# Attention factors of four edge groups at once and one-hot matrices built on GpSimd, in the second graph layer's sums

## The reference, cut to what matters

```python
def _L1_gnn_ref(h, W, a_l, a_r, src, dst):
    N, IN_FEAT, OUT_FEAT, HEADS, E = (2500, 1024, 256, 4, 40000)
    NEG_SLOPE = 0.2
    z = jnp.einsum('ni,hif->nhf', h, W)
    el = jnp.einsum('nhf,hf->nh', z, a_l)
    er = jnp.einsum('nhf,hf->nh', z, a_r)
    e = jax.nn.leaky_relu(el[src] + er[dst], NEG_SLOPE)
    m = jax.ops.segment_max(e, dst, num_segments=N)
    ex = jnp.exp(e - m[dst])
    s = jax.ops.segment_sum(ex, dst, num_segments=N)
    alpha = ex / s[dst]
    out = jax.ops.segment_sum(alpha[:, :, None] * z[src], dst, num_segments=N)
    return out.reshape(N, HEADS * OUT_FEAT)
```

## Time and profile before

| | us |
|---|---|
| median of 3 runs | 3157.28 |
| lowest and highest of them | 3145.21, 3158.06 |
| span of the profiled execution | 3172.0 |
| of it, from the first to the last product of the sums (L1508 to L1550) | 1878.5 to 2518.0 |
| busy over the whole span: TensorE, VectorE, ScalarE, GpSimd | 2750.2, 2445.8, 1667.2, 1658.5 |

### The profile page before, as it was taken

One profiled execution on the slowest core, in us unless ns is written; L12 is line 12 of the kernel. 1 busy time (PEld: TensorE's weight loads), 2 busy tenths in 40 slices (PEclk: granted clock), 3 DMA queues, 4 the chain that ended last, 5 costly groups with the idle time before them and its releaser, 6 DMA issues. The chain is left out here.

```text
span 3172.0 us, 49827 instructions
## 1 busy us (share of the span) xinstructions
PE 2750.2 (87%) x13389; PEld 2152.8 (68%) x13389; DVE 2445.8 (77%) x5315; ACT 1667.2 (53%) x3377; POOL 1658.5 (52%) x1473
## 2 busy tenths in 40 slices
PE   4999969999997998477877789999999789499997
PEld 3788734444445776355656568888888678388886
DVE  8656769999997676356666589999999986677875
ACT  3555623333334525122222259999999754366664
POOL 1788757766663562555555525555555332034333
PEclk9999989999998999789898899999999889599999
DMA  5433489999991031001010138888888854588886
GB/s 182 115 94 101 159 304 342 340 345 342 345 335 50 7 135 54 13 17 22 16 22 15 22 140 309 304 311 306 309 308 309 257 192 162 203 228 230 230 235 160
DMA packets 197470, 600.30 MB, mean 189 GB/s; under 512 B 42763, under 2 KB 52354, under 8 KB 196174
## 3 DMA queue, kind: packets, MB, share of 16 engines
q0 software_dynamic: 135040, 429.23, 42.5%
q1 hardware_dynamic: 62286, 169.29, 15.3%
HBM read 513.25 MB, written 84.95 MB: 189 GB/s over the span
## 5 line engine op out<-in xcount | busy, mean ns | idle before, releaser
L663 POOL DMA_INDIRECT g_rows<-z_rows,edge_src x704 | 731.6, 1039 | 513.4 <-PE g_totals L1550 227.7
L1132 POOL DMA_INDIRECT shared<-el_rows,edge_src x352 | 337.1, 958 | 317.3 <-DVE t_largest L1379 164.1
L1512 PE MATMUL g_sums<-g_rows,g_share 128*128 128x256 f32 x1760 | 446.0, 388 | 2.9 <-issue 1.6
L704 ACT ACTIVATE g_scaled_hi<-g_rows,edge_weight_sorted 128x1024 fp32r<-128x1024 f32 x176 | 202.6, 1151 | 361.7 <-DMA g_rows<-z_rows,edge_src 346.7
L1379 DVE TENSOR_REDUCE t_largest<-t_masked 128x4 f32<-128x512 f32 x352 | 234.4, 685 | 160.9 <-PE t_masked L1218 112.3
L718 PE MATMUL g_sums<-g_rows,g_share 128*128 128x512 f32 x704 | 333.4, 596 | 21.1 <-DMA g_rows<-z_rows,edge_src 21.1
L1512 PEld LDWEIGHTS g_sums<-g_rows,g_share 128*128 128x128 f32 x1760 | 308.8, 191 | 37.0 <-issue 2.4
L331 POOL DMA_INDIRECT edge_list<-payload,row_i x196 | 259.9, 1326 | 125.8 <-issue 116.5
L739 DVE SCALAR_TENSOR_TENSOR g_scaled_lo<-g_rows,edge_weight_sorted,g_scaled_hi 128x1024 fp32r<-128x1024 f32 x176 | 225.6, 1282 | 54.1 <-ACT g_scaled_hi L704 39.2
L1216 PE MATMUL t_masked<-t_never,t_apart 128*128 128x512 f32 x352 | 158.1, 449 | 109.0 <-DVE t_largest L1379 88.3
L1485 ACT ACTIVATE g_scaled_hi<-g_rows,g_factor 128x256 fp32r<-128x256 f32 x528 | 227.9, 494 | 15.1 <-DMA g_rows<-z_rows,edge_src 9.7
(11 more groups left out here) (407 smaller groups left out, 7553.3 us busy)
## 6 DMA issues: line engine op xcount, KB each, us to landing
e_raw<-in_L_ffn_rw_dram SPq DMA_DIRECT2D x28, 1024.0 KB
g_rows<-z_rows,edge_src POOLq DMA_INDIRECT x704
g_place_of<-place_rows SPq DMA_DIRECT2D x44, 256.0 KB
z_rows<-z_zout SPq DMA_DIRECT2D x20, 512.0 KB
x_rows<-x_all SPq DMA_DIRECT2D x20, 512.0 KB
z_rows<-t_zout SPq DMA_DIRECT2D x20, 512.0 KB
s_x<-x_rows SPq DMA_DIRECT2D x20, 512.0 KB
xn_rows<-s_rows SPq DMA_DIRECT2D x10, 1024.0 KB
```

What stands on the lines that cost most here:

```text
L663: pool.indirect_dma_start(out=r.rows[:, slot, :], out_offset=None, in_=table, in_offset=bass.IndirectOffsetOnAxis(ap=g.src[:, i * GT + q:i ...
L1132: q.indirect_dma_start(out=g.edge_el[:, n, :], out_offset=None, in_=g.el, in_offset=bass.IndirectOffsetOnAxis(ap=g.src[:, n:n + 1], axis=0 ...
L1512: t.matmul(sums[:, it.buf(2), h // 2, h % 2 * HF:(h % 2 + 1) * HF], share[:, it.buf(2), n, :], r.rows[:, it.buf(4) * GT + q, h * HF:(h + 1 ...
```

## The change

- The reads of the place broadcast stay, but the one-hot matrices `comes` are made on GpSimd, by one comparison per group (128 x 256, bf16 to fp32r), between the gathers; ScalarE's Square and Relu go. `comes` has four buffers now. GpSimd makes `comes` of group i + 4 after the gathers of group i.
- `of_edge` has two PSUM banks of four groups each. VectorE's reduction, addition, leaky relu and subtraction, and ScalarE's exponential, run once in four groups on four times the data.
- The lags grow: VectorE's step s has `goes` of s - 5 and, when that is the first of four, the scores of s - 5 to s - 2; the share and `scaled_lo` are of s - 6, the sums on TensorE of s - 7, `x_all` of s - 8. `factor` has eight buffers.
- The share of head 1, column 0, moves from VectorE to ScalarE (two and three shares become one and four).
- A turn of `in_steps` is 8 groups on TensorE and VectorE too, and ScalarE writes two turns out ahead of its loop.

```diff
-        comes = a.sb("g1_comes", [P, 2, GT, P], F32R)
+        comes = a.sb("g1_comes", [P, 4, GT, P], F32R)
-        of_edge_bank = a.psum("g1_of_edge", [P, HALF])
+        of_edge_banks = a.psum("g1_of_edge", [P, 2, HALF])
+        SCORED, SCALED, SUMMED, KEPT = AHEAD + 1, AHEAD + 2, AHEAD + 3, AHEAD + 4
...
         @block.gpsimd
-            gather_groups(nc, pool, r, g, g.z1)
+            def gather(i):
+                at_least(pool, r.multiplied, i - 3)
+                for c in range(GT):
+                    slot = i % 4 * GT + c
+                    q.indirect_dma_start(
+                        out=r.rows[:, slot, :], out_offset=None, in_=g.z1,
+                        in_offset=bass.IndirectOffsetOnAxis(ap=g.src[:, i * GT + c:i * GT + c + 1], axis=0),
+                    ).then_inc(r.gathered[slot], 16)
+            def come(i):
+                if i >= NG:
+                    return
+                if i % AHEAD == 0:
+                    pool.wait_ge(place_in[i // AHEAD % 2], (i // AHEAD // 2 + 1) * 16)
+                at_least(pool, of_edge_ready, i - 3)
+                at = i % AHEAD * GT * P
+                q.tensor_scalar(comes[:, i % 4].rearrange("p q n -> p (q n)"),
+                                place_of[:, i // AHEAD % 2, at:at + GT * P], lane[:, 0:1], None,
+                                ALU.is_equal).then_inc(comes_ready, 1)
+            for i in range(NG):
+                gather(i)
+                if i == 0:
+                    pool.wait_ge(lane_ready, 1)
+                if i < AHEAD:
+                    come(2 * i)
+                    come(2 * i + 1)
+                else:
+                    come(i + AHEAD)
...
         @block.scalar
-                    s.activation(apart[:, m, :], place_of[:, it.off // AHEAD, at:at + GT * P], ACT.Square,
-                                 bias=minus_lane[:, 0:1]).then_inc(apart_ready, 1)
...
-                    s.activation(comes[:, m].rearrange("p q n -> p (q n)"), apart[:, m, :], ACT.Relu, bias=one[:, 0:1],
-                                 scale=-1.0).then_inc(comes_ready, 1)
-                it = item(2)
+                it = item(SCALED)
...
-                    act.wait_ge(factor_ready, it.i + 1)
+                    act.wait_ge(factor_ready, it.turn(AHEAD) + 1)
...
-                    for n, q, h in ((2, 0, 2), (3, 0, 3), (4, 1, NATIVE)):
+                    for n, q, h in ((1, 0, 1), (2, 0, 2), (3, 0, 3), (4, 1, NATIVE)):
...
-                it = item(1)
-                if it:
-                    k = it.buf(4)
-                    act.wait_ge(score_ready, it.i + 1)
-                    at_least(act, r.multiplied, it.i - 3)
-                    s.activation(factor[:, k].rearrange("p q h -> p (q h)"), score[:].rearrange("p q h -> p (q h)"),
-                                 ACT.Exp).then_inc(factor_ready, 1)
-            in_steps(act, NG, 2 * AHEAD, body, lead=1)
+                it = item(SCORED)
+                if it and it.off % AHEAD == 0:
+                    f = it.buf(2 * AHEAD)
+                    act.wait_ge(score_ready, it.turn(AHEAD) + 1)
+                    at_least(act, r.multiplied, it.i - AHEAD)
+                    s.activation(factor[:, f:f + AHEAD].rearrange("p k q h -> p (k q h)"),
+                                 score[:].rearrange("p q h -> p (q h)"), ACT.Exp).then_inc(factor_ready, 1)
+            in_steps(act, NG, 2 * AHEAD, body, lead=2)
...
         @block.tensor
-                it = item(3)
+                it = item(SUMMED)
...
-                    at_least(pe, score_ready, it.i)
+                    if it.off % AHEAD == 0:
+                        at_least(pe, score_ready, it.turn(AHEAD) - 1)
...
-            in_steps(pe, NG, 4, body, lead=2)
+            in_steps(pe, NG, 2 * AHEAD, body, lead=2)
...
         @block.vector
-                it = item(4)
+                it = item(KEPT)
...
-                new, it, old = item(0), item(1), item(2)
+                new, old = item(SCORED), item(SCALED)
+                it = new if new and new.off % AHEAD == 0 else None
                 if it:
-                    dve.wait_ge(of_edge_ready, it.i + 1)
-                    st.done(v.tensor_reduce(of_node[:], of_edge.rearrange("p q (a h) -> p q h a", a=2), AX.X, ALU.add))
+                    f = it.buf(2 * AHEAD)
+                    dve.wait_ge(of_edge_ready, it.i + AHEAD)
+                    st.done(v.tensor_reduce(of_node[:], of_edge[:, f // AHEAD].rearrange("p k q (a h) -> p (k q) h a", a=2),
+                                            AX.X, ALU.add))
...
-                    shared_out(0)
+                    v.tensor_scalar(share[:, m, 0, :], goes[:, k, 0, :].bitcast(F32), factor[:, f, 0, 0:1], None,
+                                    ALU.mult).then_inc(share_v, 1)
...
-                    shared_out(1).then_inc(share_v, 1)
...
-            in_steps(dve, NG, 4, body, st, 3, lead=2)
+            in_steps(dve, NG, 2 * AHEAD, body, st, 6, lead=2)
```

More of the change, by code:

```diff
@@ L109, in turn, with in_steps @@
         return self.j * (self.unroll // count) + self.off // count
-def in_steps(eng, count, unroll, body, steps=None, per_step=0, lead=1):
+def in_steps(eng, count, unroll, body, steps=None, per_turn=0, lead=1):
     turns = count // unroll
@@ L133, in in_steps @@
         if steps:
-            steps.n = entry + (j - lead) * (unroll * per_step)
+            steps.n = entry + (j - lead) * per_turn
         for b in range(unroll):
@@ L137, in in_steps @@
     if steps:
-        steps.n = entry + (turns - 1 - lead) * unroll * per_step
+        steps.n = entry + (turns - 1 - lead) * per_turn
     for b in range(unroll):
@@ L1452, in _ @@
         def _(pool):
-            gather_groups(nc, pool, r, g, g.z1)
+            q = nc.gpsimd
+            def gather(i):
[25 more added lines that the diff above has]
+                    come(i + AHEAD)
         @block.scalar
@@ L1524, in body @@
                 if it:
-                    m = it.buf(2)
                     pe.wait_ge(comes_ready, it.i + 1)
                     pe.wait_ge(node_ready, it.i + 1)
-                    at_least(pe, score_ready, it.i)
+                    if it.off % AHEAD == 0:
+                        at_least(pe, score_ready, it.turn(AHEAD) - 1)
                     for q in range(GT):
-                        mm = t.matmul(of_edge[:, q, :], comes[:, m, q, :], node[:, it.buf(4)].rearrange("p a h -> p (a h)"),
-                                      start=True, stop=True)
+                        mm = t.matmul(of_edge[:, it.buf(2 * AHEAD) // AHEAD, it.buf(AHEAD), q, :], comes[:, it.buf(4), q, :],
+                                      node[:, it.buf(4)].rearrange("p a h -> p (a h)"), start=True, stop=True)
                     mm.then_inc(of_edge_ready, 1)
-                it = item(3)
+                it = item(SUMMED)
                 if it:
@@ L1559, in _ @@
             st.link(v.tensor_tensor(lanes[:], g.ident[:], g.iota1[:], ALU.mult))
-            st.link(v.tensor_reduce(minus_lane[:], lanes[:], AX.X, ALU.add))
-            st.done(v.tensor_scalar(minus_lane[:], minus_lane[:], -1.0, None, ALU.mult))
-            st.done(v.memset(one[:], 1.0))
+            v.tensor_reduce(lane[:], lanes[:], AX.X, ALU.add).then_inc(lane_ready, 1)
             st.link(v.tensor_copy(parts[:, :, 0, :], g.scores[:]))
@@ L1588, in body @@
                 if it:
-                    at_least(dve, factor_ready, it.i)
+                    at_least(dve, factor_ready, it.turn(AHEAD))
                     dve.wait_ge(v_done, st.n)
-                    st.done(v.tensor_tensor(score[:], g.edge_el[:, bass.ds(it.i * GT, GT), :],
+                    st.done(v.tensor_tensor(score[:], g.edge_el[:, bass.ds(it.i * GT, AHEAD * GT), :],
                                             of_node[:, :, HEADS:2 * HEADS], ALU.add))
@@ L1599, in body @@
                                                    op0=ALU.mult, op1=ALU.max))
-                def shared_out(h):
-                    return v.tensor_scalar(share[:, old.buf(2), h, :], goes[:, old.buf(4), 0, :].bitcast(F32),
-                                           factor[:, old.buf(4), 0, h:h + 1], None, ALU.mult)
                 if old:
+                    k, m, f = old.buf(4), old.buf(2), old.buf(2 * AHEAD)
                     dve.wait_ge(goes_ready, old.i + 1)
-                    dve.wait_ge(factor_ready, old.i + 1)
+                    dve.wait_ge(factor_ready, old.turn(AHEAD) + 1)
                     at_least(dve, r.multiplied, old.i - 1)
-                    shared_out(0)
+                    v.tensor_scalar(share[:, m, 0, :], goes[:, k, 0, :].bitcast(F32), factor[:, f, 0, 0:1], None,
+                                    ALU.mult).then_inc(share_v, 1)
                 if it:
@@ L1618, in body @@
                         ins = v.scalar_tensor_tensor(out=scaled_lo[:, m, cols], in0=r.rows[:, k * GT + 1, cols],
-                                                     scalar=factor[:, k, 1, h:h + 1],
```

(1 more changed line is left out.)

30 lines of the change are left out of this document (12 added, 18 removed).

## The result

The changed kernel takes 3170.6 us (median of 20 runs, 3156.03 to 3178.35) where the kernel before takes 3150.3 (median of 20 runs, 3139.95 to 3162.32): a ratio of 1.0059, 95% interval 1.0047 to 1.0070. It is slower by 20 us, where I had forecast 13 us less. The spans of the two profiled executions say nothing on this, 3167.8 after and 3172.0 before: the stage's first gather starts at 1855.3 us in the one and at 1869.3 in the other, and all code ahead of it is the same. So I compare the stage alone.

What follows compares the result with a forecast made beforehand. VectorE was taken as the bound at 3.62 us a group, TensorE next at 3.53. Over 176 groups -16, late rows +2, start +1: -13 us, so 3144 from the 3157.28 median; range 3136 to 3178, 8 in 10.

Steps and rivals of the forecast that it cites:

- What bounds the kernel before: In this stage VectorE sets the pace at 3.62 us a group; TensorE, at 3.53, waits 0.09 for it.
- VectorE's own work: On VectorE, a share removed and scores done once in four groups: 3.62 falls to 3.17 us a group.
- The price of the comparison: On GpSimd, one comparison of 256 elements taken as 0.40 us, with 0.23 and 0.75 as ends.
- GpSimd's gathers: On GpSimd, a pair of gathers with the gaps ahead of them takes 2.73 us a group.
- The holds: GpSimd and VectorE blocking each other: 0.1 us a group for VectorE (3.27), 0.2 for GpSimd (3.33).
- the phase: Comparison starts 2.7 us after the gathers start, runs when VectorE's low parts are through; late engines fall back into this timing.
- The slack of the comparison: Between the comparison's end on GpSimd and TensorE's use of it: about 0.5 us.
- The start: Before the first sums, four comparisons and a second pair of gathers: 0 to 4.3 us, taken as 1.
- Late rows: ScalarE waiting for gathered rows, as TensorE sees it: 0 to 10 us, taken as 2.
- B: Rival: dear comparison after the gathers makes GpSimd (+19 us) or VectorE (+53) the bound; 3176 to 3210 us; chance 0.2.
- Rival A: Comparison holds VectorE 0.40 us every group, 3.57 to 3.62; time 3151 to 3160; chance 0.23 together with another rival.

Runs made afterwards that it cites:

- Column 1 first: Gather of column 1 issued ahead of column 0's; ratios to kernel before: on that kernel 1.0009, changed kernel 1.006, comparison on VectorE 0.9927, scores only 0.9943.
- the scores alone: Changed kernel, but the one-hot matrices stay on ScalarE (Square and Relu) and the shares stay two and three; ratio 0.9982 to the kernel before.
- The repetition: The changed kernel run again unaltered, on the chip of three later runs; ratio 1.0036 to the kernel before, stage 664.8 us.

## Why the prediction was wrong

**The outcome.** 3170.6 us lies inside the range of 3136 to 3178, but that is no credit to the mechanism: TensorE did not become the bound, the change went the other way, and the median before was 3150.3, 7 lower than the 3157.28 that I had worked from.

**What bounds the kernel before: right.** VectorE at 3.62, with TensorE 0.09 behind it. TensorE's own pace was measured as 3.52 where it is the bound. Column 1 first, worth nothing on the kernel before, confirms that rows were not what it waited for.

**VectorE's own work: right.** 3.17 us a group had been worked out. With a comparison of its own of 0.38 us, a slot of about 0.32 by its timeline (2154.80 to 2155.12), it is busy 446 of 450 us at a pace of 3.52, which is 3.49 a group, 3.17 and 0.32, and TensorE keeps its 3.52.

**The price of the comparison: this step failed.** The sum had GpSimd at 3.33 us a group, under TensorE's 3.53, with a comparison of 0.40 us, and 0.23 and 0.75 as its ends. It is 0.91 undisturbed, beyond the upper end, and GpSimd's stream came to 3.67. I had chosen by the number of inputs, a cast at 0.88 ns an element and a select of 128 elements at 0.29 us. The two-input additions, 2.15 ns an element by the same rows, are the nearer neighbours of 2.5. And 0.75, from two inputs, had been taken as the upper end for one; no row said that one input cannot cost more.

**GpSimd's gathers: over-counted.** 2.73 us a pair had 0.30 ahead of every gather and 1.17 for the first. Behind a comparison the gap is 0.17, the comparison follows a gather after 0.03, and the first gather takes 1.02: 0.17 + 1.02 + 0.31 + 0.95 + 0.02 = 2.47. With 0.91 that is 3.38, still under TensorE's 3.53. So by this sum the price alone, though more than twice my value, would not have made GpSimd the bound.

**The holds: right for GpSimd, too low for VectorE.** I took 0.2 us for GpSimd and 0.1 for VectorE. The comparison takes 1.12 on the mean, 0.21 over its 0.91; that term was right, but it comes on top of a dear comparison. GpSimd's list by lines from 1950 to 2450 us, after:

```profile
L1458 POOL DMA_INDIRECT g_rows<-z_rows,edge_src x273 | 270.5, 991 | 72.2 <-issue 59.0 <-PE g_totals L1571 13.2
L1470 POOL TENSOR_SCALAR g_comes<-g_place_of,g_lane 128x256 fp32r<-128x256 bf16 x137 | 154.6, 1128 | 3.8
```

That is 1.98 us of gathers, 1.13 of comparison, 0.46 of gaps and 0.10 of waiting for sums: 3.67. VectorE's instructions, by their means in the stage, grow by 3 x (546 - 477) for the low parts and 2 x (354 - 287) for the one-hots, 0.34 us a group; with the share it is the 0.40 that I had given as the most. VectorE is busy for 98% of 3.67, 3.60 us a group where 3.17 had been worked out. The argument that the phase would spare it fell with the price, for a comparison of 1.1 us that starts 2.3 us after the gathers ends only as the next gather begins.

Two readings behind this term were wrong as well. From rows 8 I had concluded that one engine waits for the other's whole instruction. Here it doesn't: the comparison of 1.27 us from 2154.78 runs beside the three low parts of 2154.86 to 2156.27, and those take 0.14 us more than undisturbed. And not only the comparison holds VectorE. The one-hots of 0.68 and 0.56 us (the latter from 2154.25) end as a gather's issuing ends, as those of the kernel with the scores alone do; of the changed kernel's 78 over 0.40 us, 68 end within 0.06 us of a gather's end. The comparison queued behind may add to it, for with it one-hots are stretched that start 0.3 us into the issuing, and with the scores alone only those from 0.5 us on; the runs don't settle that. Why VectorE and GpSimd block each other for part of an instruction here is open. The rule of the Trainium skill, page "SBUF — State Buffer", section "Who interferes with whom", that VectorE's scalar operations in a two-port mode take the lock as well fits the share, 0.40 us wholly beside a comparison and 0.28 without; that the other engine is blocked for the whole instruction, as the page has it, the trace does not bear out.

**The slack of the comparison: gone with the price.** The prediction gave the comparison about 0.5 us between its end and TensorE's use of it, with 0.40 us for the comparison. This is a second way in which the price tells, beside GpSimd's own sum. One round, after:

```profile
2151.59 0.51 PE L1571 MATMUL g_totals<-g_factor,g_goes 128*128 128x4 f32 x4
...
2156.11 0.39 PE L1551 MATMUL g_of_edge<-g_node,g_comes 128*128 128x16 f32 x2
...
2159.06 0.50 PE L1571 MATMUL g_totals<-g_factor,g_goes 128*128 128x4 f32 x4
```

The sums of a group end at 2152.10. The gathers that need them start at 2152.47, the comparison behind these ends at 2156.05, TensorE takes it up at 2156.11, and ends the sums of the group two on at 2159.56: 7.46 us for two groups, 3.73 each. Over 120 groups the gathers start 0.34 us after the sums on the mean and 0.28 at the least, and the product starts 0.11 after the comparison, 0.05 at the least: each engine goes nearly as soon as the other lets it. In the kernel with the comparison ahead of the gathers the product never comes earlier than 1.95 us after the comparison's end, and GpSimd's waiting for sums is gone. How much of the loss comes by this round and how much by GpSimd's own total the runs do not separate, since that edit shortened the comparison too.

**The start: too low.** I took 1 us of 0 to 4.3; it is 7.5. GpSimd's stream after its first two gathers, after:

```profile
1858.30 1.85 POOL L1470 TENSOR_SCALAR g_comes<-g_place_of,g_lane 128x256 fp32r<-128x256 bf16 x2 [0.80 <-DMA g_place_of<-place_rows]
1860.31 1.03 POOL L1458 DMA_INDIRECT g_rows<-z_rows,edge_src  x1 [0.16 <-issue]
1861.64 0.95 POOL L1458 DMA_INDIRECT g_rows<-z_rows,edge_src  x1 [0.31 <-issue]
1862.61 1.85 POOL L1470 TENSOR_SCALAR g_comes<-g_place_of,g_lane 128x256 fp32r<-128x256 bf16 x2
```

The fourth comparison ends at 1864.5, 9.2 us after the first gather, and that is just when the first sums started in the kernel before (1878.5 - 1869.3). With the comparison on VectorE the first addition is back at 15.9 us. But with the scores alone, where ScalarE makes the matrices and GpSimd only gathers, it comes at 20.1, so 4.8 of the 7.5 us appear without a comparison on GpSimd too: the first factors need four groups' matrices, and the engine that makes them must be quick. That the gathers of groups 1 to 3 stand behind comparisons too had not been counted; what it costs is not shown apart.

**Late rows: the right cover, wrongly sized.** I took 2 us of 0 to 10. Where GpSimd is free the pace is 3.575 with the gathers in the old order and 3.520 in the new: 0.055 x 176 = 10 us. With the scores alone, where no share was moved to ScalarE, the same order is worth 0.047 us a group, so the moved share is not what makes late rows dear. In the changed kernel the term is hidden behind GpSimd.

**The rivals.** B was the one that came: its place (the instruction behind the gathers) and its mechanism are what the runs show; its point of decision, a comparison that takes over 0.80 us with its wait, was right too. Its size came near by two errors that partly cancel: comparison and waiting at 1.12 and 0.10 instead of 0.75 and 0.25, and the gathers at 2.47 instead of 2.73. The pace is 3.67, not 3.73, and the stage 13 us longer instead of 19. I had given it 0.2. Rival A, VectorE held, is in it too: 3.60 us a group for A's 3.57. The measured 3170.6 lies between the two, in the gap where I had put no case. What the sum would have given with the measured terms: 3.67 for 3.62 in some 160 groups, +8; seven instead of three last groups without the products of `of_edge`, at 3.31 us, -1 to -2; start +7.5: about 13 to 14, the stage's difference. Of the 20 us between the medians, 7 are not in the two profiled stages. The repetition had 12 in all, and the profiled stages themselves spread: 662.3, 664.8 and, with column 1 first, 665.0 for the changed kernel, 649.2 and 646.7 for the kernel before with either order of gathers. So I take the 7 us for spread between sets of runs; it isn't settled.

## What to carry to other kernels

Work moved off the bound to an engine with idle time needs a price from that engine, for that kind of instruction; if no row has one, the upper end of its cost has to be at least the dearest per-element rate seen there, and the case in which it decides deserves most of the chance when the next bound is only a few per cent away. When the best possible gain is 2.5% of a stage, every hand-over in the chain counts as much as the work: here the order of two gathers was worth 10 us and the place of one comparison in its queue 16. An instruction that is queued behind others inherits what they wait for. Batching the small instructions was the good half of this change, and it showed only when the other half was taken away.

## What the runs showed of the hardware

A comparison with a per-partition scalar, bf16 to fp32r, takes GpSimd 0.27 us and 2.5 ns an element (590 ns for 128, 911 for 256), and VectorE 0.38 us for the 256, a slot of 0.32. GpSimd and VectorE hold each other up in both directions, for part of an instruction. With comparisons on GpSimd the low parts, which have two SBUF inputs, take 546 ns on the mean for 477, and the comparison 1.12 us for 0.91; a single-input share beside a comparison takes 0.40 for 0.28. A one-hot instruction is stretched to as much as 0.68 us when it starts 0.3 us or more into a gather's issuing, and ends with it (from 0.5 us on with the scores alone). The additions from PSUM were not touched: 1214 ns on the mean before and 1216 where the comparison runs beside them (comparison ahead of the gathers). A gather that follows a comparison starts 0.17 us after it (changed kernel), one that follows a gather 0.30.
